# A sparse expert layer behind attention: rank table turned by bf16 products, last row tiles side by side, preparation moved up

## The reference

```python
# xattn: 16 heads of 32 columns, keys/values = halves of ctx, bias b, mask by length
q = split_heads(layernorm(x)) * 32 ** -0.5
w = softmax(q @ k.T + b + MASK * (1 - valid))
x = x + tanh(g_xattn) * merge_heads(w @ v)
# ffn on n = layernorm(x)
logits = n/|n| @ (centroids/|centroids|).T + n @ w_route.T      # 8 per token
gates  = softmax(where(logits >= second_largest, logits, -inf))
h      = gelu(n @ w1[e] + b1[e])                                # 512 -> 256
x = x + tanh(g_ffn) * sum_e gates[e] * (h @ w2[e] + b2[e])      # 256 -> 512
```

## Time and profile before

| | us |
|---|---|
| runs, median (lowest, highest) | 1887.98 (1885.58, 1890.13) |
| profiled execution, its own time | 1887.81 |
| span of its instructions | 1886.1 |
| last product of the attention sums starts | 1283.74 |
| last row tile's scores written | 1312.67 |
| block table complete | 1329.40 |
| first gather issued | 1341.12 |
| first rows transposed for the experts | 1353.57 |

### The profile page before, as it was taken

How to read it: one execution, slowest core, us unless ns; L and a number is a source line. 1 busy time by engine, 2 the same in 40 slices (tenths; PEclk the granted TensorE clock), 3 DMA queues, 4 the chain that set the end, 5 groups by cost and what they waited for, 6 DMA issues and landing times. The chain is left out here.

```text
span 1886.1 us, 32941 instructions
## 1 busy us (share of the span) xinstructions
PE 1729.0 (92%) x9696; PEld 1040.0 (55%) x9697; DVE 1373.5 (73%) x2997; ACT 1191.9 (63%) x2052; POOL 1250.1 (66%) x1490
## 2 busy tenths in 40 slices
PE   2699999999999999999999999996399999999997
PEld 1344555555555555555555555543277777777775
DVE  4677887877878788878787888752676676666675
ACT  4267677677676776767767767663365555555554
POOL 1258577576685775766756757562368888888887
PEclk9999999999999999999999999996599999999999
DMA  5979898899898988998989888844278887978784
GB/s 118 171 131 190 156 171 185 127 205 156 156 193 162 171 185 128 205 153 160 194 161 172 184 128 170 131 124 146 70 130 162 151 148 153 168 139 153 149 153 72
DMA packets 173067, 291.45 MB, mean 155 GB/s; under 512 B 37982, under 2 KB 42078, under 8 KB 172944
## 3 DMA queue, kind: packets, MB, share of 16 engines
q1 hardware_dynamic: 138704, 219.88, 60.3%
q0 software_dynamic: 32928, 67.68, 20.4%
q10 hardware_dynamic: 1312, 2.38, 0.8%
HBM read 127.09 MB, written 71.63 MB: 105 GB/s over the span
## 5 line engine op out<-in xcount | busy, mean ns | idle before, releaser
L1066 DVE TENSOR_REDUCE bank<-bank 128x1 f32<-128x512 f32 x1024 | 696.8, 691 | 256.8 <-PE bank L841 248.6
L700 ACT ACTIVATE prob<-bank 128x512 f32<-128x512 f32 x1024 | 592.7, 597 | 356.9 <-PE bank L829 356.0
L619 POOL TENSOR_TENSOR prob<-prob 128x512 f32<-128x512 f32 x256 | 320.3, 1281 | 326.1 <-PE bank L764 326.1
L829 PE MATMUL bank<-stB,stA 100*128 100x512 f32 x1024 | 477.2, 467 | 16.0 <-ACT prob L700 13.6
L841 PE MATMUL bank<-stA,stB 98*128 98x512 f32 x1024 | 423.3, 416 | 35.7 <-DMA stA<-regrouped_then_w 20.3
L829 PEld LDWEIGHTS bank<-stB,stA 100*128 100x128 f32 x1024 | 193.4, 189 | 248.9 <-ACT prob L700 176.4
L623 POOL TENSOR_TENSOR prob<-prob 128x512 f32<-128x512 f32 x256 | 319.5, 1278 | 0.0
L764 PE MATMUL bank<-prob,vin 128*32 128x512 f32 x2048 | 272.7, 605 | 0.7 <-ACT prob L700 0.7
L1332 POOL DMA_INDIRECT out_dram<-yout,scatter_ids x144 | 242.9, 1687 | 45.1 <-issue 41.1
L841 PEld LDWEIGHTS bank<-stA,stB 98*128 98x128 f32 x1024 | 197.8, 193 | 84.4 <-DVE bank L1066 38.9
L1302 POOL DMA_INDIRECT rows_in<-xn_rows,gather_ids x152 | 161.8, 1064 | 86.0 <-DVE rows_in L1517 45.0
(11 more groups left out here) (190 smaller groups left out, 2207.0 us busy)
## 6 DMA issues: line engine op xcount, KB each, us to landing
stB<-regrouped_then_w SPq DMA_DIRECT2D x192, 256.0 KB, 5.8
stA<-regrouped_then_w SPq DMA_DIRECT2D x183, 256.0 KB, 6.7
x_k_then_w<-in_x_dram SPq DMA_DIRECT2D x16, 1024.0 KB, 8.1
x_k_then_w<-in_ctx_dram SPq DMA_DIRECT2D x16, 1024.0 KB, 12.1
vin<-in_ctx_dram SPq DMA_DIRECT2D x16, 1024.0 KB, 9.3
xres<-in_x_dram SPq DMA_DIRECT2D x16, 1024.0 KB, 6.6
out_dram<-xres SPq DMA_DIRECT2D x16, 1024.0 KB, 7.4
xn_rows<-xn SPq DMA_DIRECT2D x64, 256.0 KB, 5.6
```

The costliest lines, as they stand in the source:

```text
L619: pool.tensor_tensor(first[:, j, :], first[:, j, :], more[:, j, :], ALU.add).then_inc(s_acc, 1)
L700: act.activation(prob_of(st, 0, u)[:, j, :], psS[j % 2][:, :], ACT.Exp).then_inc(s_exp, 1)
L829: pe.matmul(psS[j % 2][:, :], stA[0:100, g, j, kt * P:(kt + 1) * P], stB[0:100, g, j, :], start=True, stop=True).then_inc(s_qk, 1)
L1066: dve.tensor_reduce(mx[:, s // 4, s % 4:s % 4 + 1], psM[s % 2][:, :], AX.X, ALU.max).then_inc(s_mx, 1)
```

## The change

It keeps the arithmetic of attention and of the experts, and edits the passage between them:

- **Rank table.** `mask_all` becomes `masks` in bf16 with an empty tile ahead; the triangular matrices are bf16. For each expert two accumulating products have the masks as weights and the triangle as moving operand, so that the result comes out turned. `rank_t`, its copy and the eight transposes go. PE starts when the last mask is written, not when all thirteen instructions of `route` are.
- **Last four row tiles.** They leave the steps 65 to 68. ACT writes all four rows to `late_x` (in the space of `vin`), with no wait for a store between them; PE turns and scores them in four banks of their own, and VectorE copies and scores. `row_scale` of the last batch runs on VectorE.
- **Last sums.** For group 63 GpSimd adds nothing; PE sums all four parts of `prob`, 32 products for 16.
- **Table chain.** Rounding in one instruction for two (twice), the running sum of eight counts by one scan for one copy and six instructions.
- **Weights.** w2 of experts 0 to 3 is loaded in step 61, of 4 and 5 in step 62, of 6 and 7 in step 65 as before. `w2_hi` is done by ACT during the tail, in the space of `stA`; `w2_lo` of experts 0 to 3 by GpSimd, of 4 to 7 by VectorE after the first two gather lists.
- **Start of the experts.** No clearing of `rows_in`, no `f_clear`; the second program block goes, its additions are made by SP in the first; the first block's w1 is split ahead of the transposed rows; a one-element Gelu stands ahead of the loop.

```diff
-            if 0 <= n + off < groups:
+            if 0 <= n + off < (groups - 4 if off == -5 else groups):
...
@@ gpsimd
-                    if st.g() == 1 and st.on(-5):
-                        row_scale(st)
-                    if st.on(0):
+                    if st.g() == 1 and st.on(-5) and st.l <= G:
+                        row_scale(pool, st)
+                    if st.l == G:
+                        for e in range(3):
+                            w2_lo(pool, e)
+                    if st.on(0) and st.l < G - 1:
...
+                pool.wait_ge(s_ln2, LN2 * B)
+                for e in range(3, POOL_LO):
+                    w2_lo(pool, e)
@@ scalar
+                def w2_hi(e):
+                    act.wait_ge(s_qk, 16 * G)
+                    act.wait_ge(s_w2[max(e // 2 - 1, 0)], 64 if e < 4 else 32)
+                    act.activation(w2h[:, e, :, :], w2_all[:, e, :, :], ACT.Copy).then_inc(s_2hi, 1)
...
+                        if s in (0, 3) and st.l == G:
+                            for e in ((0, 1), (2, 3))[s // 3]:
+                                w2_hi(e)
...
+                act.wait_ge(s_ln2, late.batch(LN2, -5, ROW_READY))
+                act.wait_ge(s_pv, PV * (G - NT))
+                for t in range(NT):
+                    act.activation(late_x[:, t, :], xres[:, par, t, :], ACT.Identity, bias=shift2[:, t:t + 1],
+                                   scale=rsb[:, t:t + 1]).then_inc(s_xn2, 1)
+                    if t == 0:
+                        gate_exp(late)
+                for e in range(4, 6):
+                    w2_hi(e)
+                gate_exp(final)
+                for e in range(6, E):
+                    w2_hi(e)
@@ tensor
-                    pe.wait_ge(s_acc, st.count(ADDS, off, ADDS))
+                    if st.l + off < G - 1:
+                        pe.wait_ge(s_acc, st.count(ADDS, off, ADDS))
-                    for u in (0, NT - 1):
+                    for u in (0, NT - 1) if st.l + off < G - 1 else range(NT):
...
+                turn_late(0)
+                turn_late(1)
+                score_late(0)
+                turn_late(2)
+                score_late(1)
+                turn_late(3)
+                score_late(2)
+                score_late(3)
-                pe.wait_ge(s_route, ROUTE * B)
+                pe.wait_ge(s_route, ROUTE * (B - 1) + NT + 1)
+                for e in range(E):
+                    bank = psM[1] if e < 4 else psS[0]
+                    at = bank[0:TILES, (e % 4) * P:(e % 4 + 1) * P]
+                    pe.matmul(at, masks[:, 1:TILES + 1, e], up_to_row[:, :], start=True, stop=False)
+                    last = pe.matmul(at, masks[:, 0:TILES, e], later_row[:, :], start=False, stop=True)
@@ vector
+                row_scale(dve, late)
+                route_logit(late, 0)
+                row_norms(late)
+                for s in (5, 6):
+                    route(late, s)
+                dve.wait_ge(s_pv, PV * G)
+                take_late(0)
+                take_late(1)
+                route(late, 12)
+                take_late(2)
+                for s in (13, 14, 15):
+                    route(late, s)
+                take_late(3)
+                for t in range(NT):
+                    logit_late(t)
+                for s in (5, 6, 12, 13, 14, 15):
+                    route(final, s)
-                then(dve.tensor_copy(cum[:, 0, :], nblk[:, :]))
-                for k in (1, 2, 4):
-                    then(dve.tensor_copy(cum[:, 1 - src, 0:k], cum[:, src, 0:k]))
-                    then(dve.tensor_tensor(cum[:, 1 - src, k:E], cum[:, src, k:E], cum[:, src, 0:E - k], ALU.add))
-                    src = 1 - src
+                then(dve.tensor_tensor_scan(cum[:, src, :], ones[:, 0:E], nblk[:, :], 0.0, ALU.mult, ALU.add))
@@ experts
-                                pool.wait_ge(f_clear, i + 1)
-                    for i in range(2):
-                        dve.memset(rows[:, i, :, :], 0.0).then_inc(f_clear, 1)
-                    for e in range(E):
-                        dve.wait_ge(f_2hi, e + 1)
-                        dve.tensor_tensor(w2l[:, e, :, :], w2_all[:, e, :, :], w2h[:, e, :, :].bitcast(F32), ALU.subtract).then_inc(f_2lo, 1)
+                    for e in range(POOL_LO, E):
+                        w2_lo(dve, e)
```

More of the change, by code:

```diff
@@ L521, in step @@
                         sp.dma_start(w1_all[:, e, :, :], w1[e].rearrange("(k p) n -> p k n", p=P)).then_inc(s_w, 16)
-                    if st.rnd is None and 0 <= st.l - (G - 2) < E // 2:
+                    if st.l in (G - 3, G - 2, G + 1):
+                        if st.l == G - 3:
+                            i, before = turn_of(st, "TK", -1)
+                            sp.wait_ge(s_turn[i], before + 1)
+                            some = range(0, 4)
                         if st.l == G - 2:
@@ L879, in _, with turn_late, score_late @@
                 all_steps(pe, step)
+                def turn_late(t):
+                    pe.wait_ge(s_xn2, NORMAL + t + 1)
+                    for k in range(KD):
+                        last = pe.transpose((psS + psM)[t][:, k * P:(k + 1) * P], late_x[:, t, k * P:(k + 1) * P], ident[:, :])
+                    last.then_inc(l_turn, 1)
+                def score_late(t):
+                    pe.wait_ge(l_took, t + 1)
+                    for k in range(KD):
+                        last = pe.matmul((psS + psM)[t][:, 0:2 * E], late_t[:, t, k, :], routeT[:, k, :],
+                                         start=(k == 0), stop=(k == KD - 1))
+                    last.then_inc(l_lg, 1)
@@ L891, in _ @@
[L891 to L897 removed]
+                pe.wait_ge(t_dve, 2)
                 pe.matmul(psT[0][0:TILES + 1, 0:E], earlier_row[0:TILES, 0:TILES + 1], tile_count[:, :], start=True, stop=True)
@@ L1218, in flamingo_kernel @@
             f_hs = sem("gelu_split")
-            f_y = sem("out_ready")
-            f_yg = sem("out_biased")
-            f_yo = sem("out_done")
-            f_hold = sem("pool_held")
-            f_clear = sem("rows_cleared")
-            adds = [(f_y, 2 * NS), (f_yg, 2 * NS), (f_yo, 2 * NS), (f_hold, 4)]
-            with nc.Block() as block:
-                @block.sync
-                def _(sp):
-                    for start_of, count in adds:
-                        sp.sem_inc(start_of, count)
             def n_rounds(eng):
@@ L1444, in step @@
                             act.activation(hT[:, 0, m, :], gelu[:, m, :], ACT.Copy).then_inc(f_hhi, 1)
-                    act.wait_ge(s_w, 16 * 2 * E)
-                    for e in range(E):
-                        act.activation(w2h[:, e, :, :], w2_all[:, e, :, :], ACT.Copy).then_inc(f_2hi, 1)
+                    act.activation(gelu[:, 0, 0:1], ones[:, 0:1], ACT.Gelu)
+                    act.wait_ge(s_w, 16 * E)
                     rounds(act, step)
```

189 lines of the change are left out of this document (111 added, 78 removed).

## The result

| | before | changed | ratio |
|---|---|---|---|
| median of the runs (lowest, highest), us | 1888.75 (1885.58, 1890.13), 4 runs | 1863.42 (1861.10, 1865.07), 4 runs | 0.9863 [0.9848, 0.9878] |
| profiled execution, its own time | 1887.81 | 1861.90 | |
| span | 1886.1 | 1860.2 | |

The change saves 25.3 us. The forecast was 1867.9, a gain of 19.9, with a range from 1862.3: the time lies in it, near its lower end, and the profiled execution gained 25.9. The table shows where, as distances from one landmark of the seam to the next in the profiled executions.

A forecast was written before the change was run, and what follows sets the result against it. The prediction held the loop bound by GpSimd and priced the seam before it as one chain, each step worth its length. Its ten steps summed to -19.9 us, from 1887.81 to 1867.9, range 1862.3 to 1874.3.

The forecast's parts named there:

- another phase: Experts' loop: all 34 cycles take a longer form, 15.0 us each costing 29.6, to 1897.5 us; chance 0.03.
- half lost: Loop held by GpSimd: half of the seam's gain is taken back there, 1877.9 us; chance 0.04.
- Step 1: Last group's sums: 32 products for 16 cost +1.7 us, 1 more if they don't cover ScalarE's weight copies.
- Steps 2, 4, 6, 7: row_scale on VectorE, -1.3 us; PE waiting only for masks, -1.8; table chain, -1.4; one program block fewer, -0.5.
- Step 3: Last four row tiles: PE full for 10.9 us of turns and scores at the slow clock; -2.9 us.
- first rival: PE's clock rises in the tail, from the second late score through the rank products: -3.5 us, 1864.4; chance 0.20.
- Step 5: Rank products: 16 bf16 products take 2.0 us plus 0.15 for the last copy, against 7.15; -5.0 us.
- Step 8: First gather no longer waits for the clearing, 6.7 us behind its list before; -5.7 us.
- Step 9: First four gathers: first issue to PE 10.0 us for 12.45, with VectorE work beside issues; -2.4 us.
- rival of free gathers: First four gathers issue at 1.30 us each, not held up by VectorE: 1865.5 us; chance 0.11.
- Step 10: Experts' first block: w1 split ahead gives -0.6 us, the table load's removal 0 to -0.2.
- Costs nothing: SP's w2 loads in step 61 and semaphore additions: no cost, under 1 us if loads slowed the next maxima rows.

The follow-up runs named there:

- a_sums: Changed kernel with GpSimd's additions and 16 products for the last group's sums put back: 1863.53 us, ratio 0.9859 to the kernel before.
- b_again: The kernel before, unchanged, run once more for its profile: 1885.68 us in one run.
- b_stack: Kernel before with stack A and w2's high parts as one buffer of the outer scope: 1886.46 us, ratio 0.9987 to the kernel before.
- a_fp32: Changed kernel with masks and triangles in float32 instead of bf16, order of products kept: 1864.61 us, ratio 0.9868 to the kernel before.
- a_lo8: Changed kernel with w2_lo of all eight experts on GpSimd, none on VectorE: 1870.35 us, ratio 0.9867 to the kernel before.
- a_again: The changed kernel, unedited, run once more: 1870.15 us, ratio 0.987 to the kernel before.
- a_w1: Changed kernel with the first block's w1 split put back behind the first two transposed pieces: 1866.63 us, one run.

## Why the prediction was right, and by how much it was off

**The bound.** The loop of the experts kept its cycle: the last and first of its 35 holds on GpSimd are (1838.99 - 1358.14) / 34 = 14.14 us apart, for 14.13 before. What was taken ahead of the first add arrived at the end but for 0.8 us. The rivals "another phase", which ended slower, and "half lost" are out.

**Step 1, sums: right, in size and in mechanism.** I put +1.7 on the 32 products and hid ScalarE's weight copies inside them, with 0.3 us to spare. Measured +1.69, with 0.41 to spare. a_sums shows the other side of it: once the products are back at 16, the copies hold the tail by 0.98. "Cover missing", which I had in the bounds, did not happen.

**Steps 2, 4, 6, 7: right**, within 0.1 us each. The store of the gates, issued at 1307.67, did not show as a wait: VectorE began the experts 1.54 us behind the table. No run puts `row_scale`, the old late tiles or the second program block back by themselves; these terms rest on the landmarks of the traces.

**Step 3, late tiles: the term was mis-sized, 2.1 us.** I added busy times, 1.11 for a turn and 1.89 for a tile's scores, to 10.9 us. But groups of products overlap at their ends, and in the earlier trace rows each stood alone, behind a wait. In the rows of after a turn (1295.57) is followed by scores (1296.47) after 0.90 us, and these by the next turn (1298.04) after 1.57, where the busy times say 1.12 and 1.73. Three such turns, two such scores and the last pair, 3 x 0.89 + 2 x 1.56 + 3.43, make the measured 9.2 us. The other 0.35 is ScalarE's second row, which reached PE 2.55 us behind the start of the first (1295.57 - 1293.02) for 2.9 in the forecast. The clock stayed at 0.50, so the gain here is not the first rival's, though it looks like it in size.

**Step 5, rank products: right.** 0.12 us from one product to the next, for the 0.125 that I took from the row of four bf16 products; with the copy and the weights of the count product behind it the step took 2.57 for 2.15. The 7.15 us that it was set against is the slow case: 6.29 in b_again and b_stack. The upper bound, 4.4, was too low for float32, which takes 6.08 (a_fp32).

**Step 8, clearing: right**, -5.75 for -5.7, and shown by putting it back.

**Step 9, gathers: near, and its reason holds.** Issues of 1.36, 1.01, 1.64 and 1.97 us. The first two lie beside little on VectorE, the next two beside its `tensor_tensor`; where that is gone (a_lo8), the third takes 1.00, and the fourth, now beside the split of w1, 2.09. The rival of free gathers would have had 7.65 us to PE, I had 10.0, measured 9.34. The Trainium skill (SBUF — State Buffer, Who interferes with whom) would leave descriptors alone beside a `tensor_tensor`; the trace differs, by 1.64 against 1.00 us for the same gather.

**Step 10, first block: right at like clocks, and the rest luck.** Forecast 0.6 to 0.8, measured 2.07 in the pair of first traces, but 0.53 where both kernels run their products at the high clock (b_again against the changed kernel), and 0.0 between the first trace of before and a_again, whose products took 0.5 longer. The clock of those two executions gave 1.5: 1.4 in the products (5.87 us for 24 against 7.24), the rest ahead of them. The split was worth the 0.54 forecast. The table load was worth 0.1 us behind slow products and 0.4 behind fast ones, where I had at most 0.2; but from the first w2 product to the first add the changed kernel takes 10.65 us where the kernel before takes 10.22 in both its traces, which gives 0.4 back. What takes it there was not looked for.

**Attention: a step that was not in the prediction.** "Costs nothing" was all I had said of it, and it gained 2.7 us. It arises where the pipeline fills, when PE waits for the first stacks to land. The same product of the filling pipeline, one fence each, in the kernel before, in the changed kernel and in a_fp32 (b_stack has it at 81.51, after 7.39 us of waiting):

```profile
81.46 0.77 PE L841 MATMUL bank<-stA,stB 98*128 98x512 f32 x1 [7.37 <-DMA stA<-regrouped_then_w]
```

```profile
79.42 0.77 PE L907 MATMUL bank<-stack_a_then_w_hi,stB 98*128 98x512 f32 x1 [6.49 <-DMA stack_a_then_w_hi<-regrouped_then_w]
```

```profile
79.44 0.76 PE L907 MATMUL bank<-stack_a_then_w_hi,stB 98*128 98x512 f32 x1 [6.53 <-DMA stack_a_then_w_hi<-regrouped_then_w]
```

From 81.46 to 79.42 it is 2.0 us, most of the 2.7. The same transfers land sooner; queue rows (packets, MB, share of 16 engines) and issues (count, KB each, median us to landing) of the kernel before, of b_stack, and of the changed kernel:

```profile
q1 hardware_dynamic: 138704, 219.88, 60.3%
stA<-regrouped_then_w SPq DMA_DIRECT2D x183, 256.0 KB, 6.7
x_k_then_w<-in_ctx_dram SPq DMA_DIRECT2D x16, 1024.0 KB, 12.1
```

```profile
stack_a_then_w_hi<-regrouped_then_w SPq DMA_DIRECT2D x183, 256.0 KB, 6.7
```

```profile
q1 hardware_dynamic: 138704, 219.88, 57.8%
stack_a_then_w_hi<-regrouped_then_w SPq DMA_DIRECT2D x183, 256.0 KB, 5.8
x_k_then_w<-in_ctx_dram SPq DMA_DIRECT2D x16, 1024.0 KB, 9.1
```

## What to carry to other kernels

Price a chain that passes between engines by its landmarks, and PE's groups in it by the distance of their starts, not by busy times, which overlap by 10 to 20%. Ask of each clearing and each `tensor_tensor` on VectorE beside a GpSimd DMA issue what it does to that issue, and before moving work to an idle GpSimd, which short VectorE instructions it will hold. When small buffers change size, look where the large ones behind them now begin, and compare the landing times of transfers that nobody edited. Before a difference around a dense stretch of PE is put down to an edit, compare the granted clock in both traces: here it made 0.9 us in one step and 1.5 in another, and nearly all of what leaving out the Gelu seemed to cost.

## What the runs showed of the hardware that was not expected

- PE full for 9.2 us with 16-column scores and 128-column turns stayed at a granted clock of 0.50; with 18 products of 512 columns ahead of them, 5.96 us, it was 1.00 from 1294 to 1300 and 3.3 us were won, and it was back at 0.50 before the rank products.
- The first block's 24 products took 5.85 to 8.56 us in the profiles of the changed kernel and its variants, and 5.86 to 7.24 in those of the kernel before and b_stack: the same products, with another moment at which the clock rose.
- A GpSimd `tensor_tensor` of 128x1024 held an eight-element VectorE `tensor_scalar` for 2.35 us instead of 0.17.
- An indirect gather takes 1.00 us to issue alone, 1.64 to 2.43 beside VectorE's `tensor_tensor` (the fifth gather 2.43 beside it, 1.00 in a_w1 without it), 3.48 over the end of a clearing of 128x2080 and the `tensor_tensor` behind it.
- The same 138704 packets took 57.8% of the DMA engines' span instead of 60.3%, with other starts of the SBUF buffers.
